# Turning tiles off TensorE in a gated cross-attention block: three more turns by 32x32 squares and DMA, and a new order of TensorE's step

## The reference

```python
# x: (8, 512, 256), ctx: (8, 512, 256), weights 256x256, w1 256x1024, w2 1024x256
x_n  = layernorm(x)
emb  = x_n + ctx
q, k, v = emb @ wq + bq, emb @ wk + bk, emb @ wv + bv
w    = pos_bias * (abs(i - j) < 64)                 # 512 x 512
ek   = exp(k - max over rows of k);  ew = exp(w - max over columns of w)
y    = sigmoid(q) * (ew @ (ek * v)) / (ew @ ek)
a    = layernorm(y @ wo + bo + emb) * gamma + beta
ff   = relu(a @ w1 + b1) @ w2 + b2
x1   = x + tanh(g_xattn) * (layernorm(ff + a) * gamma + beta)
z    = layernorm(x1);  zp = z shifted down one row (first row 0)
r    = sigmoid((mu_r * z + (1 - mu_r) * zp) @ W_r)
kk   = relu((mu_k * z + (1 - mu_k) * zp) @ W_k) ** 2
out  = x1 + tanh(g_ffn) * r * (kk @ W_v)
```

## Time and profile before

| | |
|---|---|
| time, median of 3 runs | 468.49 us (468.48 to 469.59) |
| the profiled execution | 468.55 us, its span 466.8 us |
| granted TensorE clock | 0.996 |
| TensorE busy, products / weight loads | 443.9 us (95%) / 403.4 us (86%) |
| VectorE busy | 395.1 us (85%) |
| ScalarE busy | 241.7 us (52%) |
| GpSimd busy | 274.2 us (59%) |
| the store of the squares to DRAM, issue to landing | 2.7 us median |
| the four loads of 128 KB back, issue to landing | 2.9 to 3.0 us median each |
| turns on TensorE: norm / emb / sums | 72 / 56 / 14 products |

### The profile page before, as it was taken

The page is one execution under the profiler, slowest core; times in us unless marked ns, Lnnn a source line. Parts: engine busy times, 40 slices in busy tenths (PEclk is TensorE's granted clock), DMA queues, the critical chain, the costliest instruction groups (busy, mean ns, idle before and its releaser), DMA issues.

```text
span 466.8 us, 8151 instructions
## 1 busy us (share of the span) xinstructions
PE 443.9 (95%) x2984; PEld 403.4 (86%) x2984; DVE 395.1 (85%) x745; ACT 241.7 (52%) x378; POOL 274.2 (59%) x245
## 2 busy tenths in 40 slices
PE   7989989799999999999999999999999999999975
PEld 7769788689989898999989898999989897897975
DVE  4998878998987998888987998888977988489887
ACT  3682562735375634836375644836373634537253
POOL 2574840783578825973577825973577526853611
PEclk9999999989999999999999999999999999999999
DMA  8840410133104330234104330322103220011002
GB/s 266 277 135 6 139 61 1 46 92 135 46 10 126 119 110 0 76 105 137 47 6 131 114 113 1 101 80 90 47 1 107 74 91 0 2 47 45 1 1 91
DMA packets 30536, 35.95 MB, mean 77 GB/s; under 512 B 1952, under 2 KB 28064, under 8 KB 30496
## 3 DMA queue, kind: packets, MB, share of 16 engines
q1 hardware_dynamic: 29408, 33.85, 22.5%
q10 hardware_dynamic: 1088, 1.57, 1.0%
HBM read 24.93 MB, written 10.49 MB: 76 GB/s over the span
## 4 chain that ended last, share of the span: by engine, by line
PE 41%; DVE 21%; POOL 15%; issue 14%; ACT 5%; DMA 4%; ACTq 0%; SPq 0%; DVEq 0%; POOLq 0%
PE ps L1485 38%; DVE y L759 8%; POOL hid_lo L231 3%; POOL a_rows L498 2%; PE ps L1491 2%; DVE y L753 2%; DMA hid<-in_wo 1%; DVE emb_lo L657 1%; ACT hid_hi L1268 1%; POOL emb L498 1%; DVE xk L829 1%; POOL x_beta L498 1%; POOL xk_lo L231 1%; POOL ek_lo L231 1%; DVE xr L829 1%
## 5 line engine op out<-in xcount | busy, mean ns | idle before, releaser
L1485 PE MATMUL ps<-w_hi,hid_hi 128*128 128x256 f32 x288 | 73.2, 290 | 0.8 <-issue 0.5
L1485 PE MATMUL ps<-w_lo,hid_hi 128*128 128x256 f32 x288 | 71.9, 285 | 0.0
L1485 PEld LDWEIGHTS ps<-w_hi,hid_hi 128*128 128x128 f32 x288 | 55.2, 192 | 3.0 <-DVE y L766 1.6
L1485 PEld LDWEIGHTS ps<-w_lo,hid_hi 128*128 128x128 f32 x288 | 55.3, 192 | 0.1
L759 DVE RECIPROCAL y<-y 128x512 f32<-128x512 f32 x16 | 53.6, 3349 | 0.3
L905 DVE SCALAR_TENSOR_TENSOR hid_lo<-ps,neg_b,hid 128x512 fp32r<-128x512 f32 x60 | 41.7, 738 | 12.9 <-ACT hid L1310 12.9
L1485 PE MATMUL ps<-a_hi,w_hi 128*128 128x512 f32 x128 | 50.9, 398 | 1.3 <-DVE hid_lo L905 1.1
L1304 ACT ACTIVATE hid_hi<-ps,b 128x512 fp32r<-128x512 f32 x60 | 38.0, 685 | 27.2 <-PE ps L1485 27.2
L1485 PE MATMUL ps<-a_hi,w_lo 128*128 128x512 f32 x128 | 50.7, 396 | 0.0
L231 POOL TENSOR_TENSOR ev_lo<-res,ev_hi 128x1024 fp32r<-128x1024 f32 x8 | 19.2, 2397 | 48.2 <-ACT ev_hi L1243 48.2
L1485 PE MATMUL ps<-w_hi,hid_lo 128*128 128x256 f32 x288 | 41.9, 286 | 4.1 <-DVE hid_lo L905 3.0
(11 more groups left out here) (257 smaller groups left out, 1303.3 us busy)
## 6 DMA issues: line engine op xcount, KB each, us to landing
x_in<-in_x SPq DMA_DIRECT2D x8, 512.0 KB, 4.1
emb<-in_ctx SPq DMA_DIRECT2D x8, 512.0 KB, 4.3
x_beta<-in_x SPq DMA_DIRECT2D x8, 512.0 KB, 3.6
out<-out_sb SPq DMA_DIRECT2D x7, 512.0 KB, 2.9
room<-norm SPq DMA_DIRECT2D x6, 512.0 KB, 2.7
y<-room SPq DMA_DIRECT2D x24, 128.0 KB, 2.9
room<-hid SPq DMA_DIRECT2D x6, 512.0 KB, 2.7
hid<-room SPq DMA_DIRECT2D x24, 128.0 KB, 3.0
```

The source lines that it names most:

```text
L1485: return pe.matmul(o, s, m, start=start, stop=stop, skip_group_check=True)
```

## The change

Three more turns leave TensorE: the mid norm of batches 1 to 6 (`turn_mid_squares`, `spread_mid`), the embedding of batches 3 to 7 (`turn_emb_squares`, `store_emb`, `load_emb`), and the sums of the keys' tiles from batch 2 (a transpose at the end of `sum_keys`, `spread_sums`). Each has its own DRAM buffer. The first part is SyncE's and VectorE's new functions; `...` marks what is left out.

```diff
+            def to_room(room, blocks):
                 sp.dma_start(room.rearrange("(p n) -> p n", p=P), blocks).then_inc(room_filled, 16)
+            def from_room(square, room, landed):
                 for b in range(NB):
                     sp.dma_start(square[SQ * b:SQ * (b + 1)]..., room...[b]).then_inc(landed, 16)
...
+            def spread_sums(n):
+                sp.wait_ge(ek_rows_done, n + 1)
+                after(sp, sums_landed, sums_moved(n - 1))
+                to_room(sum_room, sums_t)
+                sp.wait_ge(room_filled, sums_stored(n))
+                sp.wait_ge(sums_lo_done, 2 * n - 1)
+                for k in range(3):
+                    sp.dma_start(sums_raw[SQ * k:SQ * (k + 1)]..., sum_room...).then_inc(sums_landed, 16)
+            def spread_mid(n):
+                sp.wait_ge(mid_turned, mid_turns(n))
+                to_room(mid_room, mid_blocks)
+                sp.wait_ge(room_filled, mid_stored(n))
+                sp.wait_ge(hid_lo_done, 2 * NQ * n)
+                from_room(mid_square, mid_room, mid_landed)
...
             def step(i, p):     # SyncE
                 if has(i + 1):
                     spread_keys(i + 1)
+                    spread_sums(i + 1)
                 if has(i + 2):
                     load_ctx(i + 2, p)
+                if mid_squares(i):
+                    spread_mid(i)
+                    sp.wait_ge(mid_landed, mid_moved(i))
+                if has(i + 2):
+                    store_emb(i + 2)
                 if has(i - 2):
                     store(i - 2)
-                load_again(i)
                 if has(i + 3):
                     load_x(i + 3)
+                if has(i + 2):
+                    load_emb(i + 2)
+                load_again(i)
                 if not is_last(i):
                     spread_fin(i - 1)
...
+            def turn_mid_squares(n):
+                dve.wait_ge(norm_done["mid"], TT * (n + 1))
+                turn_squares(mid_blocks, norm, mid_turned)
+            def turn_emb_squares(n, p):
+                dve.wait_ge(emb_done, n + 1)
...
+                turn_squares(emb_blocks, emb[p], emb_turned)
```

GpSimd takes over two low parts, `a_square_low` and `emb_square_low`, and its order changes:

```diff
             def step(i, p):     # GpSimd
+                if has(a):
+                    pool.wait_ge(norm_done["fin"], TT * (a + 1))
                 ev_low(i)
+                if has(d) and d >= FIRST_EMB:
+                    emb_square_low(pool, d)
+                finish_a(b, 1 - p)
+                if has(d):
+                    emb_plus_bo(d, 1 - p)
                 if has(a):
                     delta_of(pool, a)
+                if has(a) and is_last(i):
                     xk_low(pool, a)
                     xr_low(pool, a)
                 y_low(pool, i)
-                if has(d):
-                    emb_plus_bo(d, 1 - p)
+                if has(a) and not is_last(i):
+                    xk_low(pool, a)
+                    xr_low(pool, a)
                 if has(e):
                     stats("head", e)
...
-                finish_a(b, 1 - p)
                 x_plus_beta(b)
+                if has(a) and not is_last(i):
+                    sq_low(pool, a)
                 stats("mid", i)
+                if has(e):
+                    pool.wait_ge(norm_done["mid"], TT * (i + 1))
+                    make_emb(pool, e, p)
                 scale_a(i, p)
...
-                if has(e):
-                    make_emb(pool, e, p)
+                if has(d):
+                    ek_low(pool, d)
                 stats("ff", b)
-                if has(d):
-                    pool.wait_ge(x1_done, TT * (b + 1))
-                    ek_low(pool, d)
+                if mid_squares(i):
+                    a_square_low(pool, i)
                 stats("fin", b)
```

VectorE's order (the unchanged lines stand without a sign):

```diff
             def step(i, p):     # VectorE
-                sums_low(i, 0)
-                if has(d) and d > FIRST_EK:
+                if i < FIRST_EK:
+                    sums_low(i, 0)
+                else:
+                    hidden_low(b, 1)
+                gate_den(i, 0)
+                if d == FIRST_EK:
...
+                else:
+                    gate_den(i, 1)
+                    recip(i, 0)
+                    sums_low(i, 1)
+                recip(i, 1)
+                make_y(i)
                 if has(a):
                     mix_k(a)
-                recip(i, 1)
-                if has(a):
                     mix_r(a)
-                make_y(i)
-                if has(a):
-                    square(a)
                 if has(d):
                     key_max(d)
                 if i == 1:
                     unit_low(6)
                     unit_low(7)
                 if has(e):
                     head_stats(e)
                 if has(d):
                     turn_key_squares(d)
+                if has(a):
+                    square(a)
+                if has(d):
                     sum_keys(d)
                 hidden_low(b, 2)
                 attention_sum(i, p)
+                if not is_last(i):
+                    normalise_mid(i)
                 hidden_low(b, 3)
                 if is_last(i):
                     normalise_mid(i)
+                else:
+                    turn_mid_squares(i)
                 if has(a):
                     gate_ffn(a)
...
+                if has(d):
+                    sums_low(d, 0)
+                if has(e):
+                    turn_emb_squares(e, p)
                 ff_sum(b, 1 - p)
-                ff_stats(b, None if is_last(i) else lambda: a_low(i))
+                ff_stats(b)
                 scale_ff(b)
                 finish_x1(b)
                 fin_stats(b)
-                hidden_low(i, 0)
+                if has(d):
+                    keep_values(d)
+                    weigh_values(d)
                 if not is_last(i):
                     normalise_fin(b)
                     turn_fin_squares(b)
-                if has(d):
-                    keep_values(d)
-                hidden_low(i, 1)
+                hidden_low(i, 0)
...
```

TensorE's order:

```diff
             def step(i, p):     # TensorE
                 weigh(i, 0, 1, ek_hi, ek_lo, ek_lo_done, den_done)
-                if d == FIRST_EK:
+                if i == 1:
                     turn_emb(d, 1 - p)
+                else:
+                    add_hidden(b, 0)
+                relus_read(NQ * b + 2)
...             # num with add_hidden(b, 1)
+                if is_last(i):
+                    last_step_products(i, a, b)
+                    return
+                keys(d)
+                relus_read(NQ * b + 1)
+                hidden(b, 2)
                 if has(a):
                     ffn_k(a)
                     ffn_r(a)
                     pe.wait_ge(sq_done, a + 1)
...
                 pe.wait_ge(y_hi_done, i + 1)
                 rows_out(2, unit(1, 1), y_hi, y_lo, y_lo_done, i + 1, wo_done)
+                relus_read(NQ * b + 3)
                 hidden(b, 3)
                 if has(a):
                     ffn_v(a)
                 add_hidden(b, 2)
-                if not is_last(i):
-                    add_hidden(b, 3)
-                pe.wait_ge(norm_done["mid"], TT * (i + 1))
-                turn(2, norm, mid_turned)
...
+                add_hidden(b, 3)
+                pe.wait_ge(res_done, i + 1)
+                queries(d, 2)
+                pe.wait_ge(ek_done, DC * (d + 1))
+                if has(a):
+                    pe.wait_ge(gated_done, a + 1)
+                values(d, 1)
+                relus_read(NQ * i)
+                hidden(i, 0, DC * i)
+                pe.wait_ge(exp_q_done, DC * (d + 1))
+                hidden(i, 1)
-                if has(e):
-                    turn_emb(e, p)
-                if not is_last(i):
-                    add_hidden(i, 0)
```

More of the change, by code:

```diff
@@ L26 @@
 FAR = 64 + TT
-FIN_DVE = 3
 FIRST_DVE = 2
@@ L31 @@
 FIRST_EK = 2
+FIRST_MID = 1
+FIRST_EMB = 3
 NU = 8
@@ L133, in flamingo_gated_block @@
         KINDS = ("head", "mid", "ff", "fin")
+        VE = {"head": 2, "mid": 2, "ff": 1, "fin": 2}
         st = {k: sb(f"st_{k}", TT * HD) for k in KINDS}
@@ L203, in flamingo_gated_block @@
         gated_done, out_done = sem("gated_done"), sem("out_done")
-        ek_landed, fin_landed = sem("ek_landed"), sem("fin_landed")
+        ek_landed, sums_landed, mid_landed, emb_landed, fin_landed = (sem("ek_landed"), sem("sums_landed"), sem("mid_landed"),
+                                                                      sem("emb_landed"), sem("fin_landed"))
         room_filled = sem("room_filled")
-        rooms = [nc.dram_tensor(f"room{k}", [P * PAIR], F32, kind="Internal").ap() for k in range(2)]
+        key_room, sum_room, mid_room, emb_room, fin_room = (
+            nc.dram_tensor(f"{k}_room", [P * n], F32, kind="Internal").ap()
+            for k, n in (("key", PAIR), ("sum", DC * SQ), ("mid", PAIR), ("emb", PAIR), ("fin", PAIR)))
         last_norm_dve, last_sq_lo = sem("last_norm_dve"), sem("last_sq_lo")
@@ L1383, in step @@
                     unit_high(7)
```

(10 more changed lines are left out.)

359 lines of the change are left out of this document (217 added, 142 removed).

## The result

| | before | after |
|---|---|---|
| time, median | 468.60 us (468.48 to 469.59, 4 runs) | 509.02 us (506.29 to 511.3, 4 runs) |
| profiled execution / its span | 468.55 / 466.8 us | 508.8 / 507.1 us |
| granted TensorE clock | 0.996 | 0.963 |

The change makes the kernel 1.0855 times as long (95% interval 1.0799 to 1.0911): 40.4 us slower. I had forecast slower, by 19.2.

What follows compares the result with a forecast made beforehand. TensorE was taken as the bound, its 10.5 us saving outweighed by waits and VectorE-GpSimd meetings: +12.4 to the end of step 7's make_y, +6.8 in the last step, on 468.55 gives 487.8, say 488 us; range 466 to 501.

Steps and rivals of the forecast that it cites:

- two blocks: Both GpSimd subtractions, y_low and xk_low, get between mix_r's VectorE instructions; 2.35 us more than with one.
- one block: One 2.35 us GpSimd subtraction gets between mix_r's VectorE instructions; mix_r ends 4.9 after E, the end of make_y.
- three in all: Rival: mix_r loses both turns and finish_x1 meets a_low; middle step 58.6, 505 us; chance 0.15.
- (b): VectorE's finish_x1 meets GpSimd's a_low within 0.3 us; 2.3 us lost if a_low is first.
- Clock: Last step's 3.8 us wait for xk_hi can lower TensorE's clock; 1.5 us, left out of the sum.
- First step: hidden(0, 3) waits for hidden_low(0, 2), TensorE idle 6.5 us; E (end of make_y) of step 2 at 132.7 against 131.42.
- Step 6: Taken at 52.7 us, as it has no head statistics and no embedding to turn.
- my middle step: Period from E to E in the middle, taken as 55.2, between ends 52.15 and 58.6.
- Last step: mix_k moves behind make_y, so wo begins 12.35 after E instead of 5.5: 6.8 us later.
- Orders alone: Rival: no meeting of VectorE and GpSimd costs anything; middle step 52.15, 474 us; chance 0.20.
- (a): GpSimd's y_low and xk_low meet mix_r on VectorE after make_y; one or two subtractions of 2.35 us get between.
- point 4: Walk to the next E: period 52.15; 2.0 of 2.5 us per step given back as waits for xk_lo and a_lo.

Runs made afterwards that it cites:

- m1: Separate test kernel, not the layer: VectorE instructions with two SBUF inputs beside GpSimd subtractions; 9.2 us each alone, 17.7 together.
- e1: Changed kernel with GpSimd waiting for the end of mix_r before y_low in steps 2 to 6; 494.0 us.
- e6: e5 with GpSimd's order after the wait for mix_r changed to xk_low, xr_low, y_low; 482.5 us.
- e4: Changed kernel with the last step's mix_k ahead of the second reciprocal and mix_r ahead of make_y, as before the change; 505.3 us.
- e10: Changed kernel with eight zero-adding products filling TensorE's wait between ffn_k and ffn_r in steps 2 to 6; 507.0 us.
- e2: Changed kernel with GpSimd waiting for the end of finish_x1 before a_low in steps 1 to 6; 515.7 us.
- e5: e1 with a_low of batches 1 to 6 moved from GpSimd to VectorE, between scale_ff and finish_x1; 490.2 us.
- e3: Changed kernel with both GpSimd waits, for mix_r as in e1 and for finish_x1 as in e2; 504.2 us.
- e7: e6 with e4's last-step mixing, and in step 1 unit_low(6), unit_low(7) later and batch 1's mid norm earlier; 472.9 us.
- e9: e7 with GpSimd's x_plus_beta and a_rows bias moved off the mid statistics, and one fin norm tile back on ScalarE; 470.4 us.

## Why the prediction was right in direction and too low by 21 us

- **"One or two of GpSimd's subtractions get between mix_r's. One: mix_r ends at 4.9 ... Two: 2.35 more."** This is the step that failed. mix_r ended at 257.55, 6.9 after E, in each of steps 2 to 6: two blocks. y_low started 1.17 after E as forecast, but xk_low was ready behind it, and by m1 each of two queued instructions lets one through. The earlier trace rows showed this pattern; I took one block and gave three in all a chance of 0.15. That rival (E of step 7 at +30, time 505) is what came: +32.4 and 509. Its middle step of 58.6 was 58.0; some of that agreement is luck, as its sum has no term for the clock.
- **What a block costs.** The two add 4.3 to mix_r. e1 gives 15.0 us for both, 3.0 a step, since xk_lo is then later; how much of the 3.0 is the clock that no longer falls stays open. e6 gives 7.7 more for xk_low's place, which I had at 1.0 a step.
- **"(b) ... 2.3 lost if a_low is first, none if it is 2 us off."** Half right. It is lost in steps 2 to 6 (3.8 for 1.7). In step 1 it hangs on tenths: 1.67 in the changed kernel's trace, where the sum rows had met make_emb just before (2.64 for 0.42), 3.8 to 3.9 in e1, e4 and e10. And being 2 us off is not free: e2 lost 6.7 us by it, through TensorE's longer wait and the clock behind it. With (b) gone at no delay, 3.8 us in all come back, net of a_low on VectorE.
- **Clock.** I had named it for the last step and left its 1.5 us out. It fell in each of steps 2 to 6 too (0.53 over 3.6 us in step 4). Where e5 and e3 run the same step with and without a fall, it costs 1.5; in the changed kernel itself its price is not shown, as in e10 the time won ran into another meeting. I had no term for it.
- **First step.** TensorE waited 6.1 for hidden_low(0, 2) (6.5 forecast), then 2.9 more for a_hi, which I had not; E of step 2 came 2.1 later than forecast. The clock of this step was 0.87 (0.97 before the change); where it was 0.94, in e1 and e5, the step took 53.4 and 52.9, near the 52.7 that I had. e7 shows that most of both waits can be had back.
- **Step 6.** 59.4 for 52.7. I had taken 2.5 off my middle step for the head statistics and the turn of the embedding. The two blocks and (b) are in it in full; scale_ff took 2.87 for 1.70 in a meeting with ek_low, and, with the head statistics gone, VectorE waits 1.43 for the keys' exponentials and 1.36 for the sum rows, which on ScalarE stand behind the copy of the fin norm. e7 still leaves step 6 and what follows 4.4 us longer than before the change (129.5 for 125.1); which of the waits in it is worth how much stays open.
- **Last step.** +7.9 for +6.8; wo 13.6 after E for 12.35. All of this is there when ffn_k ends: xk_lo is ready 4.9 after E for 4.4, as GpSimd's subtraction met mix_r (2.81 for 2.35), and ffn_k's products ran at the clock of 0.52. e4 returned 3.8 us.
- **"Orders alone: ... 474."** No run has the forecast's orders without (a) and (b) and nothing else changed. The nearest, e5, which delays xk_lo for it, is at 490. e7 to e9, with xk_low's place and both ends mended as well, are at 470 to 473, and their period is 52.7 to 53.5 for my 52.15. So point 4 is right that the gain is given back, and wrong in how: the wait for xk_lo is gone there and that for a_lo is 0.2 to 1.8, while TensorE's busy time fell by 6.5 us in e9 (443.9 to 437.4) and not by 10.5. Where the other 4 are no run shows.
- **A slip.** VectorE's new load of 47.1 starts from 46.5, where the earlier trace rows has 45.9. Nothing hung on it.
